# Feed-forward weights: split in 32 chunks during the expert stage and read back in every feed-forward unit

## What is computed

```python
x = x + L0_ffn(layernorm(x))     # experts: F_DIM 352, top 2 of 8, silu(g) * u, weights by softmax
x = x + L1_xattn(layernorm(x), ctx)   # sim = (p kv) kv^T, normalised, softmax
h = silu(x_n @ w_gate) * (x_n @ w_up)          # w_gate, w_up [512, 2048]
h = of each 4 neighbours the 2 of largest magnitude, others 0
x = x + h @ w_down                             # w_down [2048, 512]
```

## Time and profile before

| | |
|---|---|
| median of 3 runs | 1087.94 us (1084.15 to 1089.82) |
| profiled execution | 1088.75 us, its span 1087.1 us |
| granted clock of TensorE, mean | 0.935 |
| busy: TensorE, weight loads | 964.4 us (89%), 805.5 us (74%) |
| busy: VectorE, ScalarE, GpSimd | 666.1, 390.2, 301.0 us (61%, 36%, 28%) |
| read from and written to HBM | 118.6 and 48.0 MB |
| w_scratch | 36 + 36 fetches, 16 + 16 stores |

### The profile page before, as it was taken

The page is one execution under the profiler, slowest core; times in us unless marked ns, Lnnn a source line. Parts: engine busy times, 40 slices in busy tenths (PEclk is TensorE's granted clock), DMA queues, the critical chain, the costliest instruction groups (busy, mean ns, idle before and its releaser), DMA issues.

```text
span 1087.1 us, 15614 instructions
## 1 busy us (share of the span) xinstructions
PE 964.4 (89%) x4627; PEld 805.5 (74%) x4628; DVE 666.1 (61%) x1439; ACT 390.2 (36%) x682; POOL 301.0 (28%) x370
## 2 busy tenths in 40 slices
PE   4996539999999996547788999999999999999997
PEld 3883338999999995336566888888888888888886
DVE  6986834442444422783579696885876858664446
ACT  4876224433434322332353353242432333321221
POOL 0466023332332310423363443121320411101120
PEclk8998759999999999558989999999999999999999
DMA  8178135452353321512775644474353662444751
GB/s 331 55 152 223 39 118 198 159 169 77 123 195 127 109 68 49 214 56 88 290 261 183 253 155 161 159 241 156 114 156 118 208 218 78 133 142 156 226 140 55
DMA packets 64156, 167.33 MB, mean 154 GB/s; under 512 B 7648, under 2 KB 7776, under 8 KB 62944
## 3 DMA queue, kind: packets, MB, share of 16 engines
q0 software_dynamic: 28160, 79.71, 24.5%
q1 hardware_dynamic: 35936, 86.88, 22.5%
HBM read 118.59 MB, written 47.98 MB: 153 GB/s over the span
## 4 chain that ended last, share of the span: by engine, by line
PE 45%; DVE 8%; DMA 2%; ACT 2%; POOL 2%; issue 1%; ACTq 0%; DVEq 0%; SPq 0%; POOLq 0%
PE ps L77 15%; PE ps L79 15%; PE ps L78 15%; DVE raw L2616 1%; PE ps L1878 1%; DVE f_hid L2632 1%; POOL f_w L1444 1%; DMA moe_rows<-y_scratch,slot 1%; DMA raw<-in_ffn_dn 1%; DVE x L2224 1%; DMA raw<-in_ffn_gu 1%; DVE f_stats L2234 0%; POOL f_w L1439 0%; DVE x L2651 0%; PE ps L2106 0%
## 5 line engine op out<-in xcount | busy, mean ns | idle before, releaser
L77 PE MATMUL ps<-f_x_lo,f_w 128*128 128x512 f32 (+1 forms) x520 | 206.2, 397 | 15.6 <-DVE f_hid L1494 9.0
L78 PE MATMUL ps<-f_x_hi,f_w 128*128 128x512 f32 (+1 forms) x520 | 204.5, 393 | 0.0
L79 PE MATMUL ps<-f_x_hi,f_w 128*128 128x512 f32 (+1 forms) x520 | 204.4, 393 | 0.0
L77 PEld LDWEIGHTS ps<-f_x_lo,f_w 128*128 128x128 f32 x520 | 100.0, 192 | 38.6 <-issue 9.8
L1494 DVE TENSOR_TENSOR f_hid<-moe_rows,ps 128x512 f32<-128x512 f32 x64 | 43.8, 684 | 129.1 <-PE ps L79 109.5
L79 PEld LDWEIGHTS ps<-f_x_hi,f_w 128*128 128x128 f32 x520 | 99.9, 192 | 20.6
L78 PEld LDWEIGHTS ps<-f_x_hi,f_w 128*128 128x128 f32 x520 | 100.1, 193 | 20.1
L1488 ACT ACTIVATE moe_rows<-ps 128x512 f32<-128x512 f32 x64 | 38.2, 597 | 206.8 <-PE ps L79 206.7
L77 PE MATMUL ps<-gu_w_lo,m_xT_hi 128*128 (+1 forms) x312 | 106.0, 340 | 4.5 <-DVE m_xT_lo L1735 4.4
L77 PE MATMUL ps<-f_w,kv_c_hi 128*128 128x512 f32 x256 | 102.8, 402 | 2.3 <-DVE x L2651 2.3
L78 PE MATMUL ps<-f_w,kv_c_lo 128*128 128x512 f32 x256 | 101.8, 398 | 0.0
(11 more groups left out here) (342 smaller groups left out, 1902.7 us busy)
## 6 DMA issues: line engine op xcount, KB each, us to landing
f_w<-w_scratch POOLq DMA_DIRECT2D x36, 1024.0 KB, 6.6
f_w<-w_scratch POOLq DMA_DIRECT2D x36, 512.0 KB, 5.7
w_scratch<-f_w SPq DMA_DIRECT2D x16, 1024.0 KB, 6.4
raw<-in_moe_gu SPq DMA_DIRECT2D x32, 352.0 KB
y_scratch<-m_y SPq DMA_DIRECT2D x39, 256.0 KB
raw<-in_ffn_gu SPq DMA_DIRECT2D x16, 512.0 KB
w_scratch<-f_w SPq DMA_DIRECT2D x16, 512.0 KB, 4.2
raw<-in_moe_dn SPq DMA_DIRECT2D x24, 256.0 KB
```

Source lines behind the costliest of these rows:

```text
L77: eng.matmul(out, lhs_hi, rhs_lo, start=start, stop=False)
L78: eng.matmul(out, lhs_lo, rhs_hi, start=False, stop=False)
L79: return eng.matmul(out, lhs_hi, rhs_hi, start=False, stop=stop)
```

## The change

All 16 weight chunks, each in two halves (32 pieces of 128x768 columns: `CHUNKS`, `CW`), are split during the expert stage, one in each body from tile 1 to 32. In body g SyncE issues the load of piece g behind the result's store and the reload, waits for the subtraction of the piece before it, and stores that one's hi and lo (768 KB). ScalarE rounds it (`chunk_hi`) behind `result`; GpSimd subtracts (`split_chunk`) behind `split_down`. There are two buffers of each kind, and the stage's loop has seven rounds and ten tiles written out. All 13 sets are then fetched from w_scratch by GpSimd; loads, copies, subtractions and stores of weights leave the last block. In First the fetches stand between the small GpSimd powers, `later.fetch(0, 0)` moves behind `rstd(1, 0)`, `key_lo(3)` behind `fnorm(1)`, and `dve_add(0, 0)` to the end. In `ffn` all calls of `load_*`, `keep_*`, `act_gate_up`, `act_down`, `pool_gate_up` and `pool_down` go.

```diff
-KEPT = Q
+CHUNKS, CW = 2 * Q * RQ, 3 * D // 2
+LOOPS = (CHUNKS - 1) // 4
...
     def fetch_gate_up(self, pool, s, r):
-        pool.wait_ge(self.kept_gu[r], 16 * KEPT)
-        pool.wait_ge(self.products, RQ * (FIRST[s] - 1) + r + 1)
+        if s >= 1:
+            pool.wait_ge(self.products, RQ * (FIRST[s] - 1) + r + 1)
...
     def pe_gate_up(self, pe, n, r):
-        if SPLIT[n] < KEPT:
-            pe.wait_ge(self.gate_up_lo, RQ * SPLIT[n] + r + 1)
-        else:
-            pe.wait_ge(self.got_gu[r], 16 * (SPLIT[n] - KEPT + 1))
+        pe.wait_ge(self.got_gu[r], 16 * (SPLIT[n] + 1))
...
@@ moe, buffers @@
+        pre_raw = sb("pre_raw", [P, 2, CW])
+        pre = sb("pre", [P, 2, 2, CW], F32R)
...
-            with eng.Fori(0, (REAL - 1) // 4) as i:
+            with eng.Fori(0, LOOPS) as i:
...
@@ moe, SyncE, body(g, j, i) @@
                     with sp.If((entry & MORE) != 0):
                         reload((entry & (NEXT - 1)).with_bounds(min_val=1, max_val=E - 2))
+                    if not isinstance(g, int) or g < CHUNKS:
+                        load_chunk(g, j, i)
+                    if not isinstance(g, int) or g <= CHUNKS:
+                        sp.wait_ge(pre_lo, g + 1)
+                        sp.dma_start(chunk_pair(outer["w_store"], i, j), pre[:, k, :, :].bitcast(F32)
+                                     ).then_inc(pre_kept[k], 16)
+
+                def load_chunk(g, j, i):
+                    c = (j + 1) % 2
+                    sp.wait_ge(pre_lo, g)
+                    sp.dma_start(pre_raw[:, c, :], chunk(dram["ffn"], i + (j + 1) // 4, (j + 1) % 4)
+                                 ).then_inc(pre_ld[c], 16)
...
@@ moe, GpSimd @@
+                def split_chunk(g, k):
+                    pool.wait_ge(pre_hi, g)
+                    pool.tensor_tensor(pre[:, k, 1, :], pre_raw[:, k, :], pre[:, k, 0, :].bitcast(F32), ALU.subtract
+                                       ).then_inc(pre_lo, 1)
...
                     with pool.If((entry & NEXT) != 0):
                         split_down(number(entry), other(entry))
+                    if not isinstance(g, int) or g <= CHUNKS:
+                        split_chunk(g, j % 2)
...
@@ moe, ScalarE @@
                     result(g - 1, 1 - k, 2 * i + j // 2 + 1)
+                    if not isinstance(g, int) or g <= CHUNKS:
+                        chunk_hi(j % 2, 2 * i + j // 2 + 1)
+
+                def chunk_hi(k, loads):
+                    act.wait_ge(pre_ld[k], 16 * loads)
+                    act.wait_ge(pre_kept[k], 16 * loads)
+                    act.copy(pre[:, k, 0, :], pre_raw[:, k, :]).then_inc(pre_hi, 1)
...
@@ First, GpSimd @@
+        u.fetch_gate_up(pool, 0, 0)
         rstd(0, 0)
-        u.pool_gate_up(pool, 0, 0)
+        u.fetch_gate_up(pool, 0, 1)
         rstd(0, 1)
-        later.fetch(pool, 0, 0)
+        u.fetch_gate_up(pool, 0, 3)
         rs(0)
...
+        pool.wait_ge(self.sim_done, TB)
+        u.fetch_gate_up(pool, 0, 2)
         rstd(1, 0)
-        u.pool_gate_up(pool, 0, 1)
+        later.fetch(pool, 0, 0)
         rstd(1, 1)
+        for r in range(RQ):
+            u.fetch_down(pool, 0, r)
         later.fetch(pool, 0, 1)
...
@@ First, VectorE @@
-        key_lo(3)
         o_lo(1)
...
         stats(1, 1)
+        fnorm(1)
+        key_lo(3)
+        lo(1, 1)
         self.later.dve_add(dve, 0, 0)
-        fnorm(1)
-        lo(1, 1)
...
@@ ffn, GpSimd @@
-                for r in range(2, RQ):
-                    u.pool_gate_up(pool, 0, r)
-                    slot_work(r - 1)
+                for r in range(1, RQ):
+                    u.fetch_gate_up(pool, 1, r - 1)
+                    slot_work(r)
```

More of the change, by code:

```diff
@@ L1353, in __init__ @@
         sem = outer["sem"]
[L1354 to L1358, removed]
+        self.store = outer["w_store"].rearrange("t p s (k n) -> t p s k n", k=3)
+        self.got_gu, self.got_dn, self.got_last = (
+            [sem(f"{tag}{name}{r}") for r in range(RQ)] for name in ("got_gu", "got_dn", "got_last"))
         self.gates, self.products = sem(tag + "gates"), sem(tag + "products")
@@ L1548, in pipeline, with chunk, chunk_pair @@
         def pipeline(eng, body):
-            with eng.Fori(0, (REAL - 1) // 4) as i:
+            with eng.Fori(0, LOOPS) as i:
                 for j in range(4):
                     body(4 * i + j + 1, j, i)
-            i = (REAL - 1) // 4
-            for j in range((REAL - 1) % 4):
-                body(4 * i + j + 1, j, i)
+            for g in range(4 * LOOPS + 1, REAL):
+                body(g, (g - 1) % 4, (g - 1) // 4)
+        def chunk(store, i, j):
+            t = 2 * i + j // 2
+            at = slice(t, t + 1) if isinstance(t, int) else bass.ds(t, 1)
+            return store[at].rearrange("o p n -> (o p) n")[:, CW * (j % 2):CW * (j % 2) + CW]
+        def chunk_pair(store, i, j):
+            t = 2 * i + j // 2
+            at = slice(t, t + 1) if isinstance(t, int) else bass.ds(t, 1)
+            return store[at].rearrange("o p s n -> (o p) s n")[:, :, CW * (j % 2):CW * (j % 2) + CW]
         def is_last(g):
@@ L1612, in _ @@
                 split_down(1, slice(1, 2))
+                pool.sem_inc(pre_lo, 1)
                 pipeline(pool, body)
-                pool.wait_ge(got[REAL % 4], 16 * (REAL // 4 + 1))
+                for k in range(2):
+                    pool.wait_ge(pre_kept[k], 16 * (1 + CHUNKS // 2))
                 for k in range(2):
@@ L2376, in starts, with new @@
             return n < UNITS and FIRST[SPLIT[n]] == n
-        def made(n):
-            s = (SPLIT[n],) if starts(n) else ()
-            return (s, ()) if n < UNITS and SPLIT[n] < KEPT else ((), s)
+        def new(n):
+            return (SPLIT[n],) if starts(n) else ()
         with nc.Block() as block:
@@ L2467, in _ @@
                             slot_work(6 * n + r + 1)
-                for s in made(LAST)[1]:
+                for s in new(LAST):
                     for r in range(RQ):
@@ L2703, in build @@
             "ps": ctx.enter_context(nc.psum_tensor("ps", [P, 8, 512], F32)),
-            "ld_gu": [sem(f"ld_gate_up{r}") for r in range(2)],
-            "ld_dn": [sem(f"ld_down{r}") for r in range(RQ)],
             "pool_const": sem("pool_const"),
```

146 lines of the change are left out of this document (22 added, 124 removed).

## The result

The changed kernel takes 1097.22 us (median of five executions, 1096.58 to 1099.06). Beside it on the same chip the ratio to the kernel before is 1.0094, with a 95% interval of 1.0070 to 1.0118: slower by 0.9%, where 1083 was forecast. The profiled execution took 1097.86 us, with a span of 1096.2 (before 1087.1).

A forecast was written before the change was run, and what follows sets the result against it. TensorE was taken to bound the expert stage and 600 to 1060 us, VectorE First. Units -22.9, First -6.6 and added wait +24.5 sum to -5.0, giving 1083 us, range 1069 to 1099.

The forecast's parts named there:

- The units: Feed-forward units: removing splits closes TensorE gaps (16.9 us) and restores its clock (6.0 us), together -22.9 us.
- First: Opening of the last block: removing loads and a split frees the first adds and the score instruction, -6.6 us.
- The copies and subtractions: Expert stage: ScalarE's 32 chunk copies and GpSimd's 32 subtractions fit in idle time, costing nothing.
- The added wait: Five expert-stage tiles with a reload: late chunk load delays TensorE's down product, 4.9 us each, +24.5 us.
- the clock term: Behind each of five reload gaps: TensorE's slower granted clock costs 1.4 us besides the 3.5 us gap.
- Loop edges: Expert-stage tile loop: two rounds fewer, priced at 0 to -1 us and taken as 0.
- The queue as a rival for ordinary tiles: SyncE's queue fills; loads landing over 8 us after issue make ScalarE wait in 27 other tiles: 1110, chance 0.15.
- the forecast's own sum: Whole kernel: -22.9 for the units, -6.6 for First, +24.5 for the added wait, together -5.0 us.
- the 0.18 for a slower kernel: Chance of a slower kernel, from 1093.4 us: 0.05 from the small gain plus 0.13 from the queue.
- the small gain: Units 0 and 1: VectorE's own order keeps the gaps, -12 instead of -22.9, so 1094; chance 0.18.
- the full queue: Rival of SyncE's queue filling, ScalarE waiting in ordinary expert-stage tiles: sum +22, 1110; chance 0.15.

The follow-up runs named there:

- e7: Kernel before the change with only the change's reordering of First (key_lo, dve_add and later.fetch moved); 1087.82 us beside 1088.82, ratio 0.9990.
- e4b: Changed kernel with every chunk load and store replaced by its semaphore count, copies and subtractions kept, units fetching unsplit weights from a same-size input; 1057.82 us.
- e5: Changed kernel with the chunk's load and store ahead of the expert reload and GpSimd's chunk subtraction ahead of its down split; 1071.36 us.
- e10: Changed kernel with the chunk's load issued between the wait for GpSimd's down split and the three down-weight loads; 1080.34 us.
- e3: Changed kernel with only the chunks' 768 KB stores left out, fetches reading an input of the same size; 1092.04 us.
- e9: e8 with the tile loop written out in full; 1069.42 us.
- e8: Changed kernel with four raw chunk buffers in place of two, each load issued two tiles earlier, every engine's order kept; 1070.86 us.
- e1: Changed kernel with SyncE issuing the next chunk's load before the expert reload instead of behind it; 1072.19 us.
- e11: e9 with three buffers in place of two for the split chunk that the store reads; 1059.66 us, ratio 0.9741 to the kernel before.
- e6: e5 with the tile loop written out in full; 1069.70 us.

## Why the prediction was wrong

- **The units, -22.9: right** (-22.8). The 6.65 us gap was to shrink to 1.8 and the one of 0.54 to stay; 1.75 and 0.53 are what the trace shows.
- **First, -6.6: right in kind** (-8.5): the first add, the pair of adds and the score instruction moved as worked out. e7 shows that moving `dve_add` and `key_lo` in the kernel before gave nothing (its First takes 63.4 us, against 63.8). Where the other 1.9 us come from no run shows.
- **The copies and subtractions, 0: right**, shown by e4b (tiles +0.8 us against before). In the other order of e5 they did cost: GpSimd's subtraction met VectorE's.
- **The added wait, 3.5 us of gap and 1.4 of clock, five times 4.9: mis-sized, and this turned the sign.** The mechanism, its place, its five occurrences, the issue 1.7 us behind the down loads and the 2.3 us from the landing to TensorE are all as written. The step that failed is "behind the 0.79 MB of down weights I take 3.2": that is the landing with nothing just ahead, which e10 measures at 3.3. Behind the down loads it was 5.35 in the tile shown, 5.3 to 5.6 in all five. A gap of 5.0 (24.8 / 5) took the place of 3.5, so +7.3 us. With it the clock term failed: 1.4 fits the gap of 4.2 us of the kernel before (row below: 0.83, so 1.4; the earlier trace rows show 1.6 behind the 3.45 us gap that it was said to be like), while in the kernel after it was 1.7 behind 4.0 and 4.5, and between 2.4 and 3.0 behind 5.2 to 5.6: another +4.7. Both terms lie within the bounds named (6 us, and 40 for the sum); the landing taken was the lower end of the landings shown, although the load had 0.79 MB just ahead of it. (The first two gaps are the short ones at the same landing: there the load goes out 0.8 and 0.3 us after ScalarE wants the chunk, in the last three tiles 1.4 to 1.6 us after.)

```profile
568.27:576.27 8.00, 8.00 (x33) 6.79 (x34) 6.46 (x4) 2.54 (x3) 5.97 (x4) 0.83 0.65 192
```

- **Loop edges, 0: wrong**, a second step that failed, and a smaller one. "Two loop rounds fewer, 0 to -1" looked at how many jumps there are and not at what one costs beside the stores. A round tile is 0.85 us longer, so +3.4 for the first four; e3 (no stores, 28.1) and e9 beside e8 (no jump, 27.9 against 31.8) show that it needs both the stores and the jump.
- **The queue as a rival for ordinary tiles: not so.** Outside the reloads only two tiles waited for a load, 1.6 and 0.6 us, without a gap of TensorE; the landing median is 3.3, and the longest, 6.3, is under the 8 us from which that rival counted. But e1 (for a load) and e8 (for a store) show the same kind of wait one tile behind the reload.
- Those three terms are 7.3 + 4.7 + 3.4 = 15.4 of the 17.2 us missed in the expert stage. Of the 1.8 left, 1.0 is the sixth jump, whose tile is 8.03 instead of 7.00 us; the rest is spread.

So the direction turned on one estimate. With 5.35 for 3.2 and nothing else changed, the forecast's own sum is -5.0 + 5 x 2.15 = +5.8, and 1094; with the measured gaps and clock it is -5.0 + 12.0 = +7.0, and 1095. The measured 1097 lies inside the wide range of 1069 to 1099, but that is luck and not the reasoning: the 0.18 for a slower kernel stood on the small gain and the full queue, and neither came. The larger price of the added wait was within its own bounds, of which the top alone (+40) gives 1098, and had no chance of its own.

## What to carry to other kernels

A transfer added to a queue's order inherits every wait that stands ahead of it there: place it by what can block the queue, or give it buffers enough that its place doesn't matter. Price its landing with the bytes that are just ahead of it in the queue, not with that of loads that had nothing ahead; here that difference was 2 us in each of five places, and TensorE's slower clock behind the longer gap added nearly one more. And of a chain of buffers each has to be deep enough: with deeper loads alone the wait went to the store (e8, and e9 without the loop), and the third store buffer released it (e11).

## What the runs showed of the hardware

- **A pause at the loop's jump that depends on DMA stores.** Every fourth tile is about one us longer with 768 KB stores beside a loop (31.3 and 31.8 us for four tiles), and not without the stores (28.1, 28.5) or without the loop (27.9). The Trainium skill ("Runtime: NRT & Kernel Launch", Instruction fetch mechanics) says that a taken branch outside the window of code held forces a fetch by DMA. The trace does not bear this out as the cause here: no packet on the instruction queues is recorded between 192 and 400 us of the kernel after, though four of the pauses lie there. In straight code there are such packets, as in the first two rows below, of e6 from 260 to 330 us. What goes with the pauses is the load on the DMA engines. During those of the kernel after (0.45 to 1.0 us) their share is 0.81 to 0.98, during the three longest of e8 (2.0, 1.7 and 1.4 us) 1.03, 1.04 and 0.98, and during e11's two in straight code 1.04. The last two rows show one pause of the kernel after and the longest of e8 (columns as in the table of stages). What the jump waits for in the looped kernels stays open; no run tried it alone.

```profile
q8 instruction: 4, 0.07, 0.4%
q14 instruction: 7, 0.06, 0.3%
...
225.12:225.99 0.87, 0.00 (x1) 0.01 (x1) 0.87 (x3) 0.83 (x2) 0.00 (x0) 1.00 0.91 220
...
305.39:307.35 1.96, 0.00 (x0) 0.01 (x1) 0.00 (x0) 0.59 (x1) 0.48 (x1) 1.00 1.03 413
```

- **Loss behind a gap grows with it.** The granted clock over the next 8 us was 0.83 behind a gap of 4.2 us (kernel before), 0.79 behind gaps of 4.0 and 4.5 us, and 0.62 to 0.70 behind 5.2 to 5.6, with TensorE busy all the while. So (1 - clock) x 8 is 1.4 to 1.7 us behind the shorter gaps and 2.4 to 3.0 behind the longer.
- **The traffic that one core moves.** 415 GB/s over 4 us (e11), loads from HBM and stores to it together. The 358 GB/s per core for the HBM side that the Trainium skill gives ("DMA: Bandwidth & Descriptors", Where 436 GB/s comes from) was again no bound in this program of one core.
